# A reordered residual on VectorE and two reordered projections on TensorE in a transformer block with 16 samples

## What is computed

```python
def adaln(x, t, w, b):
    emb = t @ w + b
    scale, shift = jnp.split(emb, 2, axis=-1)
    return layernorm(x) * (1.0 + scale) + shift

h1 = adaln(x, t, norm1_w, norm1_b)
x = mha(h1, h1, attn1_wq, attn1_wk, attn1_wv, attn1_wo, attn1_bo) + x      # 16 heads of 64
h2 = adaln(x, t, norm2_w, norm2_b)
x = mha(h2, context, attn2_wq, attn2_wk, attn2_wv, attn2_wo, attn2_bo) + x # 77 context rows
h3 = adaln(x, t, norm3_w, norm3_b)
x = glu_ff(h3, ff_w1, ff_b1, ff_w2, ff_b2) + x
...
x = x + block(_layernorm(x), cond, ctx)        # the first layer
x = x + mixture_of_experts(_layernorm(x))      # the second: 7 routed experts, top 2, logits from _layernorm(x)
x = x + slot_attention(cond, ctx, _layernorm(x))
x = x + top1_experts(_layernorm(x))
```

## Time and profile before

| | |
|---|---|
| median of 3 runs | 942.78 us (941.45 to 943.51) |
| profiled execution | span 942.8 us, the same as the median to the digit shown |
| TensorE (PE) busy | 803.7 us, 85% of the span, 6173 matmuls |
| VectorE (DVE) busy | 568.8 us, 60% |
| ScalarE (ACT) busy | 540.2 us, 57% |
| GpSimd (POOL) busy | 360.0 us, 38% |
| chain that ended last | PE 55%, DVE 20%, issue 9%, POOL 6%, ACT 6% |

### The profile page before, as it was taken

How to read it: one execution, slowest core, us unless ns; L and a number is a source line. 1 busy time by engine, 2 the same in 40 slices (tenths; PEclk the granted TensorE clock), 3 DMA queues, 4 the chain that set the end, 5 groups by cost and what they waited for, 6 DMA issues and landing times.

```text
span 942.8 us, 18988 instructions
## 1 busy us (share of the span) xinstructions
PE 803.7 (85%) x6173; PEld 673.0 (71%) x6173; DVE 568.8 (60%) x1941; ACT 540.2 (57%) x1147; POOL 360.0 (38%) x559
## 2 busy tenths in 40 slices
PE   5899899999999999999987588999978786861693
PEld 5777787888878888788876456999746565651693
DVE  2576887677866668776575352333558787885012
ACT  2565676667766677666754222333448888851362
POOL 1233454333333333332656150566422222226363
PEclk9897999999999999999998789999855979795697
DMA  9699111001010101000100131888600000001574
GB/s 284 230 314 342 70 37 37 15 1 50 2 37 1 51 1 37 15 1 37 48 27 20 45 105 40 245 249 243 209 7 1 1 0 1 1 1 37 152 208 126
DMA packets 43275, 78.50 MB, mean 83 GB/s; under 512 B 5339, under 2 KB 28587, under 8 KB 42651
## 3 DMA queue, kind: packets, MB, share of 16 engines
q1 hardware_dynamic: 39691, 70.09, 23.8%
q0 software_dynamic: 3488, 7.20, 2.2%
HBM read 63.98 MB, written 30.13 MB: 100 GB/s over the span
## 4 chain that ended last, share of the span: by engine, by line
PE 55%; DVE 20%; issue 9%; POOL 6%; ACT 6%; DMA 2%; SPq 2%; DVEq 0%; ACTq 0%; POOLq 0%
PE bank L899 5%; PE bank L627 5%; PE bank L689 5%; PE bank L652 4%; PE bank L642 3%; DVE sb_smax L1396 3%; PE bank L633 3%; PE bank L677 3%; DVE sb_row_sum L1406 3%; PE bank L907 3%; PE bank L661 3%; PE bank L1008 2%; PE bank L1016 2%; DVE sb_st_all L1704 2%; PE bank L718 2%
## 5 line engine op out<-in xcount | busy, mean ns | idle before, releaser
L1881 POOL TENSOR_TENSOR sb_expd<-sb_expd,sb_rden 128x512 f32<-128x512 f32 (+1 forms) x128 | 112.4, 878 | 259.4 <-DVE sb_rden L1410 259.3
L1396 DVE TENSOR_REDUCE sb_smax<-bank 128x4 f32<-128x512 f32 (+1 forms) x128 | 74.1, 579 | 64.3 <-PE bank L652 39.7
L1973 POOL TENSOR_TENSOR sb_rstd_all<-sb_rsq_all,sb_halves 128x4 f32<-128x4 f32 x44 | 45.2, 1026 | 133.5 <-DVE sb_rsq_all L1711 133.5
L677 PE MATMUL bank<-sb_eye,sb_expd 128*128 128x128 f32 (+1 forms) x512 | 77.5, 278 | 5.7 <-POOL sb_expd L1881 5.2
L1118 ACT ACTIVATE sb_expd<-sb_shifted 128x512 f32<-128x512 f32 (+1 forms) x128 | 69.8, 545 | 18.9 <-DVE sb_shifted L1399 17.9
L677 PEld LDWEIGHTS bank<-sb_eye,sb_expd 128*128 128x128 f32 (+1 forms) x512 | 59.7, 145 | 26.8 <-issue 13.5
L1406 DVE TENSOR_REDUCE sb_row_sum<-sb_expd 128x4 f32<-128x512 f32 (+1 forms) x128 | 73.0, 570 | 9.4 <-ACT sb_expd L1118 9.4
L1112 ACT ACTIVATE sb_probT<-bank 128x512 f32<-128x512 f32 (+1 forms) x128 | 74.3, 590 | 7.2 <-PE bank L677 6.9
L1399 DVE TENSOR_TENSOR sb_shifted<-bank,sb_smax 128x512 f32<-128x512 f32 (+1 forms) x128 | 75.0, 586 | 4.4
L627 PE MATMUL bank<-sb_h1T,sb_watt 128*128 128x128 f32 x512 | 72.1, 287 | 4.7 <-DMA sb_watt<-att_w 2.3
L689 PE MATMUL bank<-sb_probT,sb_v 128*64 128x128 f32 (+1 forms) x1024 | 71.7, 283 | 5.0 <-issue 3.4
(11 more groups left out here) (256 smaller groups left out, 1917.2 us busy)
## 6 DMA issues: line engine op xcount, KB each, us to landing
sb_up_w<-gate_up SPq DMA_DIRECT2D x38, 384.0 KB
rows_b<-pad_b SPq DMA_DIRECT2D x1, 8775.0 KB, 53.6
rows_a<-pad_a SPq DMA_DIRECT2D x1, 7670.0 KB, 27.9
sb_up_w<-w1b SPq DMA_DIRECT2D x23, 256.0 KB
sb_v<-v_all SPq DMA_DIRECT2D x16, 308.0 KB
v_all<-sb_v_rows SPq DMA_DIRECT2D x9, 512.0 KB, 2.6
sb_blk_x<-rows_a SPq DMA_DIRECT2D x38, 65.0 KB, 3.3
sb_watt<-att_w SPq DMA_DIRECT2D x4, 512.0 KB, 6.3
```

The source lines that it names most:

```text
L677: mm = pe.transpose(trans[u % 2][0:n, h, :], expd[:, (units_before(i) + u) % EXP_RING, h, 0:n], eye[:, :])
L1396: dve.tensor_reduce(smax[:, u % 2, :], s_in, X, ALU.max).then_inc(max_done, 1)
L1881: pool.tensor_tensor(e, e, rden[:, u % 2, :].unsqueeze(2).broadcast_to([P, QH, n]), ALU.mult).then_inc(norm_done, 1)
```

## The change

In the table, `v1_0` and `zT` leave the place ahead of the last transposes' products (step 10) and come in step 11, in the order `zT`, `v1_0`, ahead of `logit`. On VectorE, the residual of `wo2` with its waits goes to the head of step 2, ahead of unit 2's maximum; the moments of `xb` stay where they were.

```diff
     (("wo1",), ("g2_2", "ffout")),
     ((), ("hT",)),
-    ((), ("v1_0", "zT")),
-    (("logit",), ()),
+    ((), ()),
+    (("zT", "v1_0"), ("logit",)),
 ]
...
                 for k in range(N_STEPS):
+                    if k == AT["wo2"] and "C" in S:
+                        dve.wait_ge(xab_ready, c + 1)
+                        residual(i, "wo2", xb[:, :], tile(x0b, c))
                     if scored(k):
                         softmax_in(i, scored(k)[0], scored(k)[2])
                     if summed(k) and k != AT["sums"]:
                         softmax_sums(i, summed(k)[0], summed(k)[2])
                     if k == AT["wo2"] and "C" in S:
-                        dve.wait_ge(xab_ready, c + 1)
-                        residual(i, "wo2", xb[:, :], tile(x0b, c))
                         variances("B", c, [(2, xb[:, :], zB, z_ready["B"])])
```

## The result

| | before | with the change |
|---|---|---|
| median of 6 runs | 943.14 us (941.45 to 947.19) | 951.62 us (947.14 to 953.97) |
| profiled execution: its own time, span | not on record, 942.8 us | 947.14 us, 945.2 us |

The ratio is 1.0075, with a 95% interval of 1.0049 to 1.0101. It is estimated from all executions together and so isn't the quotient of the two medians, which would be 1.0090. By the ratio the change costs about 7 us, by its interval 4.6 to 9.5. The profiled execution is the fastest of the six, at a mean granted clock of 0.915; four of the others have 0.906 and one 0.912. Wherever both are on record, an execution's time is 1.8 to 2.0 us above its span, so that the span before has the digits of the median is chance.

A forecast was written before the change was run, and what follows sets the result against it. TensorE's queue order was taken as the bound (busy 288.4 of 296 us). Forecast: 942.8 + 5.7 (3.9 steady, 1.8 other iterations) - 0.8 (residual) = 947.7 us, chance 0.60, range 944.5 to 951.0.

The forecast's parts named there:

- the +4.9 us of the forecast: Whole kernel: +5.7 us from the new table order, less 0.8 us from moving VectorE's residual.
- The first rival: End of iteration 2: the products' stand makes TensorE's clock fall once more, costing 3 us, 950.7 in all; chance 0.20.
- The stand in iterations 4 to 14: TensorE's products wait 0.90 us for ScalarE's copy of unit 7 in iteration 8; +3.9 us over eleven iterations.
- The term of 0.42 per iteration: In iteration 8 `logit` begins at 291.56 in place of 291.14, 0.42 us later.
- No weights loaded ahead: TensorE doesn't load the products' weights during their stand; loading ahead would make the sum up to 1.5 us smaller.
- The residual: VectorE, step 2: moving `wo2`'s residual into idle time wins 0.8 us of the 1.5 us waited for `xb`.
- The 0.42 in iteration 12: `k1_1` waits for `rank`'s copy, which VectorE makes 0.42 us earlier, winning that time.
- 0.13 each: Three short waits of `k1_1` for `wo2`'s bank: unit 1's transpose moves from 300.70 to 300.57, limited by GpSimd's product.
- The rival in which VectorE's lead is passed on in every iteration: TensorE gains 0.42 us in each of 14 iterations, 5.9 us, cancelling the loss: 942.6 us; chance 0.13.
- Iterations 1 to 3: Copies of `hT` come between those of units 6 and 7, so their ends cost +0.9, +0.5 and +0.2 us.
- Iterations 15 and 16: Products run inside `zT`'s wait, -0.3 us; then `wo2` of iteration 17 waits longer for `oTB`, +0.5 us.

The follow-up runs named there:

- the three comparisons of the whole change: The unedited change against the kernel before, first measurement and two repeats on other chips: ratios 1.0075, 1.0052 and 1.0058.
- the version with `v1_1` behind: Against the kernel before: `v1_0` ahead of the products, `zT` and `v1_1` (moved from step 7) behind them, VectorE's residual moved: ratio 0.9960, 956.22 us.
- the table alone: Against the kernel before: only the new table order, VectorE's residual left in its old place: ratio 1.0041, 963.38 us.
- the residual alone: Against the kernel before: only VectorE's residual moved, the table left as before: ratio 0.9987, 958.79 us.
- chips A and C: Two of three chips used for follow-ups; the unedited change against the kernel before gave ratios 1.0052 (962.71 us) and 1.0058 (952.02 us) there.
- chips A and B: Two of three chips used for follow-ups; the kernel before has medians of 958.98 and 959.34 us there.

## Why the prediction held, step by step

The sign and the mechanism held, and the steady part nearly in size. Against the +4.9 us of the forecast the three comparisons of the whole change gave about +7.1, +5.0 and +5.5. The first median, 951.62, lies just above the upper end of the range, 951.0; as a ratio the forecast is 947.7 / 942.78 = 1.0052, which is inside all three intervals, in the first near its lower end. The first rival's 950.7 is 1.0084, which is inside the first and the third. So the whole time doesn't decide between the two; the traces do.

- **The stand in iterations 4 to 14: shown, a little smaller.** The transposes are issued in 0.93 us (289.84 to 290.77 in the version with `v1_1` behind). So in iteration 8 their last issue was at 293.23, the products began 0.90 behind it, as forecast, and `logit` 2.95, where 2.96 was forecast. The term of 0.42 per iteration, with the waits for `zC` set off, was to give some 3.6 over ten iterations; the table alone gave 3.06. An ordinary iteration takes 0.37 more and not 0.42. Two small parts make up the difference: `logit` starts 3.05 behind the start of the last transpose in place of 2.65, so 0.40 later, and the first scores follow it after 0.29 in place of 0.32. The last two iterations lose only 0.1, because their waits for `zC` were longer before (0.48 and 0.51).
- **No weights loaded ahead: shown.** The load of the products' weights begins with the products, behind 0.96 us without a load. The Trainium skill, TensorE: Matmul & The Clock Gate, "Part 2: What happens when you issue a matmul", has loads pulled ahead of matmuls in flight; this trace shows none pulled ahead of the wait in front of its group: here the load's own row names `probT` as what it waited for.
- **The residual: the size failed.** Forecast -0.8, measured -0.39 (over the ten iterations, which hold all four waits). The 0.42 in iteration 12 came as 0.33, and iterations 7, 8, 10, 11 and 14 each lost some 0.05. The step that failed is "0.13 each" for the three short waits. In the run of the residual alone, iterations 5, 9 and 13, which held them, didn't get shorter at all: the transposes wait for GpSimd until the same time as before. The 0.33 that was won in iteration 6 was no term of the sum: it is the wait for `zB`, which the prediction did not look at. The rival in which VectorE's lead is passed on in every iteration is refuted by the same run: 0.39 us in ten iterations, not 4.2.
- **Iterations 1 to 3.** The ordinary stands were forecast at +0.9, +0.5 and +0.2. At the clock of 1.00 the end of iteration 1 costs 1.0 us (from `wo1` of iteration 1 to the first score of iteration 2: 10.70 in the change and 10.69 with the table alone, against 9.68 and 9.67 in the two undisturbed profiles of before). The ends of iterations 2 and 3 cost 0.6 together.
- **Iterations 15 and 16: shown.** -0.33 against -0.3, and +0.42 against +0.5.
- **The clock.** Its case stood as a rival at 0.20, and the stretch at the end of iteration 2 is in every profile of the change. But the rival had it caused by the products' stand, and in two of the three it began ahead of that stand. From `wo1` of iteration 1 to `logit` of iteration 4 it takes 107.34, 106.79 and 107.84 us in the three profiles of the change, and 102.16 and 102.18 in the two of before without a stretch at the lower level. That is about 5 us, of which the stands are 1.6 and the clock some 3 to 4, near the 3 of the rival. The forecast left out two things that balance it in part: before, iteration 1 has such a stretch in one profile of three, at 105.34 us in all; and at the end the change wins. From `logit` of iteration 14 to that of iteration 17 it is 67.4, 68.5 and 69.7 us before, and 64.7, 67.05 and 64.4 now, where +0.2 was forecast. It is the clock there too, which fell before behind the stand of 1.78 for `zC`.

Added up at the full clock, the stands of the change are 1.6 (iterations 1 to 3), 0.3 (iteration 4), 2.7 (the ten) and 0.1 (15 and 16): 4.7 us against the forecast's 4.9, and near the +5.0 and +5.5 of chips A and C. So the forecast's steps are right nearly in full, but for the residual. That the clock's loss in front and its gain at the end nearly cancel was forecast nowhere; that the total came so near is in this part luck, and the first result with its +7.1 shows how far it can be off. That the stretches come from the new order isn't settled. The four profiles against three speak for a tendency; that they begin ahead of the stand in most cases, occur without it, and a stand occurs without them, speaks against it. No run here separates it, since each profile is one execution. It would also have to be known how often the clock falls in executions without a profile; their mean granted clock was 0.9016 before and 0.9022 with the change on chip A, and 0.9079 and 0.9058 on chip C.

## What to carry to other kernels

When one engine is the bound, lay its work at a point of hand-over in the new order, piece by piece, together with the copies that each piece waits for: a filler covers only one of two chains of copies, and moving it moves the stand. Before a wait is taken away ask what is due next to it on another engine; here it was GpSimd's product, and what the earlier residual won stood again in front of the transposes. And where two chains need cover and there is one filler, look for a second filler elsewhere in the loop (here `v1_1`), which was worth more than either order.

## What the runs showed of the hardware

The steady stretch of 296 us repeats within 0.06 us from trace to trace, on different chips, while the whole execution differs by 16 us between chips (943 to 959 us for the kernel before) and by 6 us and more between executions on one.

The difference between chips is mostly not the clock. From `logit` of iteration 17 to the end the eight traces from chips A and B take 413.5 to 418.9 us and the six others 403.1 to 405.7. All eight have a stand of ScalarE of 9.8 to 13.1 us that begins some 18 us behind that `logit`, and the six have none over 6.1 there. It is here in the residual alone:

```profile
569.24 0.60 ACT L1151 ACTIVATE sb_hid<-bank 128x512 f32<-128x512 f32 x1 [10.39 <-issue]
```

The profile doesn't show what it waits for, and the cause stays open.

From one execution to the next it varies where TensorE's granted clock falls. A fall near the ends of iterations 1 and 2 lasted some 3.4, 7 or 10 us. In the first layer falls came at the end of or behind stands of 1.5, 1.8 and 3.1 us with little work around them (1.80 us busy of 4 in the first), but not every time: behind 2.14 and 2.28 us there was none. On the Trainium skill: TensorE: Matmul & The Clock Gate, "Why this matters for your kernels", warns only of idle gaps longer than the stands of 1.5 and 1.8 us. The rows show falls behind these shorter ones too.
